# Cross-attention values on one Trainium2 core: four heads per product, 512 columns wide, with one set of split value weights

## The reference

```
qh = (q_in @ wq + bq)                      # h = norm(x)
kh = (kv_in @ wk + bk);  vh = (kv_in @ wv + bv)   # kv_in = context
kh = concat(kh, bias_k); vh = concat(vh, bias_v)  # one extra key per head
weights = softmax(qh kh^T / sqrt(128))
out = concat_heads(weights @ vh) @ wo + bo
```

## Time and profile before

| what | value |
|---|---|
| median of 3 runs | 1978.76 us (1978.57 to 1981.2) |
| the profiled execution's own time | 1977.81 us |
| its span | 1975.7 us |
| mean granted TensorE clock | 0.974 |
| TensorE busy | 1875.9 us, 95% |
| VectorE, ScalarE, GpSimd busy | 56%, 53%, 50% |

### The profile page before, as it was taken

One profiled execution on the slowest core, in us unless ns is written; L12 is line 12 of the kernel. 1 busy time (PEld: TensorE's weight loads), 2 busy tenths in 40 slices (PEclk: granted clock), 3 DMA queues, 4 the chain that ended last, 5 costly groups with the idle time before them and its releaser, 6 DMA issues.

```text
span 1975.7 us, 39304 instructions
## 1 busy us (share of the span) xinstructions
PE 1875.9 (95%) x15088; PEld 1551.0 (79%) x15088; DVE 1113.9 (56%) x2104; ACT 1044.2 (53%) x1945; POOL 996.6 (50%) x1140
## 2 busy tenths in 40 slices
PE   7999999988897899999999999999999998999999
PEld 5777779534454788899999999999999987977788
DVE  4566656389989654444454444454444455755654
ACT  3565543434343656665665656556566554345532
POOL 6777731366654543654544544545454434347630
PEclk9999999889998999999999999999999999999999
DMA  6000010000000222232232232232232210000000
GB/s 236 2 2 2 2 57 1 1 0 1 1 1 11 91 81 75 83 104 83 82 106 82 81 107 82 81 107 82 81 102 87 81 60 22 22 29 16 2 11 33
DMA packets 61847, 108.11 MB, mean 55 GB/s; under 512 B 7008, under 2 KB 42336, under 8 KB 60256
## 3 DMA queue, kind: packets, MB, share of 16 engines
q1 hardware_dynamic: 60784, 103.38, 16.7%
q10 hardware_dynamic: 880, 2.22, 0.3%
HBM read 103.47 MB, written 2.10 MB: 53 GB/s over the span
## 4 chain that ended last, share of the span: by engine, by line
PE 84%; DVE 7%; issue 4%; POOL 3%; ACT 2%; DMA 0%; DVEq 0%; SPq 0%; ACTq 0%; POOLq 0%
PE banks L862 18%; PE banks L891 9%; PE banks L934 9%; PE banks L627 7%; PE banks L644 7%; PE banks L466 7%; PE banks L923 6%; PE banks L904 4%; PE banks L475 3%; PE banks L548 2%; PE banks L523 2%; PE banks L505 2%; PE banks L534 2%; PE banks L912 1%; PE banks L460 1%
## 5 line engine op out<-in xcount | busy, mean ns | idle before, releaser
L1983 POOL TENSOR_TENSOR w_lo<-w2ring,w_hi 128x512 fp32r<-128x512 f32 x128 | 176.1, 1376 | 254.9 <-ACT w_hi L1128 254.9
L2067 POOL TENSOR_TENSOR wo_lo<-wo_ring,wo_hi 128x256 fp32r<-128x256 f32 x128 | 94.6, 739 | 254.6 <-ACT wo_hi L1337 254.6
L1808 DVE TENSOR_REDUCE nmax<-banks 128x4 f32<-128x260 f32 x128 | 54.3, 424 | 280.2 <-PE banks L904 280.2
L1794 DVE TENSOR_TENSOR v<-banks,dbv 128x512 f32<-128x512 f32 x128 | 88.5, 692 | 201.6 <-PE banks L891 200.7
L1337 ACT ACTIVATE wo_hi<-wo_ring 128x256 fp32r<-128x256 f32 x128 | 53.3, 417 | 197.6 <-PE banks L934 197.5
L934 PE MATMUL banks<-wo_hi,c_hi 128*128 128x256 f32 x512 | 145.5, 284 | 4.4 <-DVE c_lo L1801 4.4
L934 PE MATMUL banks<-wo_lo,c_hi 128*128 128x256 f32 x512 | 145.4, 284 | 0.0
L934 PE MATMUL banks<-wo_hi,c_lo 128*128 128x256 f32 x512 | 145.3, 284 | 0.0
L1324 ACT ACTIVATE k<-banks,cols 128x512 f32<-128x512 f32 x128 | 88.1, 688 | 79.4 <-PE banks L862 79.4
L923 PE MATMUL banks<-PT,v 128*128 128x128 f32 x1024 | 125.3, 276 | 3.4 <-issue 3.4
L923 PEld LDWEIGHTS banks<-PT,v 128*128 128x128 f32 x1024 | 120.3, 192 | 3.8 <-issue 3.8
(11 more groups left out here) (235 smaller groups left out, 5525.1 us busy)
## 6 DMA issues: line engine op xcount, KB each, us to landing
w2ring<-in_w SPq DMA_DIRECT2D x128, 384.0 KB, 4.1
b2ring<-in_b SPq DMA_DIRECT2D x128, 128.0 KB, 4.5
wo_ring<-in_wo SPq DMA_DIRECT2D x128, 128.0 KB, 4.3
mlp_w<-in_mlp SPq DMA_DIRECT2D x6, 1024.0 KB, 7.1
wl<-in_wres SPq DMA_DIRECT2D x1, 2688.0 KB, 9.0
X<-in_x_in SPq DMA_DIRECT2D x4, 512.0 KB, 11.1
wb<-in_wres SPq DMA_DIRECT2D x2, 1024.0 KB, 10.8
ctxT<-in_ctx_in SPq DMA_DIRECT2D x4, 512.0 KB, 19.8
```

The costliest lines, as they stand in the source:

```text
L1794: V.tensor_tensor(v2[:, :, 2 * half:2 * half + 2, :].rearrange("p s i d -> p i s d"), held(("v2", p, half))[:, :].rearrange("p (i s d) -> ...
L1983: G.tensor_tensor(w2_lo[:, n % 2, :], w2ring[:, n % HR, 0:2 * KT * P], w2_hi[:, n % 2, :].bitcast(f32), ALU.subtract).then_inc(S["l2_wlo"], 1)
L2067: G.tensor_tensor(wo_lo[:, n % 2, :], wo_ring[:, n % WR, :], wo_hi[:, n % 2, :].bitcast(f32), ALU.subtract).then_inc(S["l2_wolo"], 1)
```

## The change

Values are now computed for four heads at a time (HV = 4), in the iterations with n % 4 == 0. The moving operand is 512 columns wide, so that each of the four tiles of tokens fills one bank with six matmuls. v2 becomes four tensors, one per tile of tokens, two of them placed in memory that layer 2 leaves free. There is one set of wv_hi and wv_lo, for four heads, in the same memory as the two sets before. dbv is made four heads ahead rather than two. VectorE reads four banks in one iteration of two, and the waits are recounted.

```diff
+HV = 4
-        v2 = view(at("v2", A + 13584, 2 * TOK), "p (s t d) -> p s t d", s=2, t=NT)
+        v2 = [view(at(f"v2_{i}", w, HV * P), "p (s d) -> p s d", s=HV) for i, w in
+              enumerate((A + 13584, A + 14096, masks_at + 1024, masks_at + 1536))]
-        wv_hi, wv_lo = (view(at(n, M + 2048 + 1024 * i, 2 * KT * 2 * P, f32r), "p (s k h d) -> p s k h d", s=2, k=KT, h=2)
+        wv_hi, wv_lo = (view(at(n, M + 2048 + 1024 * i, KT * HV * P, f32r), "p (k h d) -> p k h d", k=KT, h=HV)
...
 TensorE, values(n)
-                        c, p = n // H2 % CHUNKS, n // 2
-                        pe.wait_ge(S["l2_wvlo"], n + 2)
-                        for half in range(2):
-                            b = take(pe, ("v2", p, half), "l2_v", 2 * p + half + 1)
-                            for i in (2 * half, 2 * half + 1):
-                                pairs = [(x, y, k) for x, y in SPLIT for k in range(KT)]
-                                for x, y, k in pairs:
-                                    last = mm(b[:, i % 2 * D:(i % 2 + 1) * D], (ctx_hi, ctx_lo)[x][:, c, k, i * P:(i + 1) * P],
-                                              (wv_hi, wv_lo)[y][:, p % 2, k].rearrange("p h d -> p (h d)"),
-                                              start=(x, y, k) == pairs[0], stop=(x, y, k) == pairs[-1])
+                        c, v = n // H2 % CHUNKS, n // HV
+                        pe.wait_ge(S["l2_wvlo"], n + HV)
+                        pairs = [(x, y, k) for x, y in SPLIT for k in range(KT)]
+                        for i in range(NT):
+                            b = take(pe, ("v2", v, i), "l2_v", NT * v + i + 1)
+                            for x, y, k in pairs:
+                                last = mm(b, (ctx_hi, ctx_lo)[x][:, c, k, i * P:(i + 1) * P],
+                                          (wv_hi, wv_lo)[y][:, k].rearrange("p h d -> p (h d)"),
+                                          start=(x, y, k) == pairs[0], stop=(x, y, k) == pairs[-1])
                             last.then_inc(S["l2_v_mm"], 1)
 TensorE, weigh(n)
-                        pe.wait_ge(S["l2_v"], 2 * (n // 2) + 2)
+                        pe.wait_ge(S["l2_v"], NT * (n // HV + 1))
-                            last = mm(out, v2[:, n % 2, i, :], PT2[:, n % 2, i].rearrange("p r q -> p (r q)"), start=True, stop=True)
+                            last = mm(out, v2[i][:, n % HV, :], PT2[:, n % 2, i].rearrange("p r q -> p (r q)"), start=True, stop=True)
 TensorE and VectorE, the loop
-                        values(n)
+                        if n % HV == 0:
+                            values(n)
 ScalarE, value_weights_hi(n)
-                    p = n // 2
-                    if p >= 2:
-                        act.wait_ge(S["l2_v_mm"], 2 * (p - 1))
+                    if n >= HV:
+                        act.wait_ge(S["l2_v_mm"], NT * (n // HV))
 VectorE, values(n)
-                        dve.wait_ge(S["l2_dbv"], n + 2)
+                        dve.wait_ge(S["l2_dbv"], n + HV)
-                        for half in range(2):
-                            dve.wait_ge(S["l2_v_mm"], 2 * p + half + 1)
-                            V.tensor_tensor(v2[:, :, 2 * half:2 * half + 2, :].rearrange("p s i d -> p i s d"),
-                                            held(("v2", p, half))[:, :].rearrange("p (i s d) -> p i s d", i=2, s=2),
-                                            dbv.unsqueeze(1).to_broadcast([P, 2, 2, P]), ALU.add).then_inc(S["l2_v"], 1)
+                        for i in range(NT):
+                            dve.wait_ge(S["l2_v_mm"], NT * v + i + 1)
+                            V.tensor_tensor(v2[i], held(("v2", v, i)).rearrange("p (s d) -> p s d", s=HV), dbv, ALU.add).then_inc(S["l2_v"], 1)
 GpSimd, bias_values(n)
-                        if n >= 2:
-                            pool.wait_ge(S["l2_v"], 2 * (n // 2))
-                        G.tensor_tensor(dbv[:, n % 2, :], ...
+                        if n >= HV:
+                            pool.wait_ge(S["l2_v"], NT * (n // HV))
+                        G.tensor_tensor(dbv[:, n % HV, :], ...
 GpSimd, start of cross2
                     for n in range(2):
                         bias_key(n)
+                    for n in range(HV):
                         bias_values(n)
 GpSimd, the loop
-                            if head + 2 < NH:
-                                bias_values(head + 2)
+                            if head + HV < NH:
+                                bias_values(head + HV)
```

More of the change, by code:

```diff
@@ L292, in build @@
         k2 = view(at("k2", A + 12544, 2 * NB * KX), "p (s b k) -> p s b k", s=2, b=NB)
-        v2 = view(at("v2", A + 13584, 2 * TOK), "p (s t d) -> p s t d", s=2, t=NT)
+        v2 = [view(at(f"v2_{i}", w, HV * P), "p (s d) -> p s d", s=HV) for i, w in
+              enumerate((A + 13584, A + 14096, masks_at + 1024, masks_at + 1536))]
         PT2 = view(at("PT2", A + 14608, 2 * NT * P), "p (s i r q) -> p s i r q", s=2, i=NT, r=2)
-        wv_hi, wv_lo = (view(at(n, M + 2048 + 1024 * i, 2 * KT * 2 * P, f32r), "p (s k h d) -> p s k h d", s=2, k=KT, h=2)
+        wv_hi, wv_lo = (view(at(n, M + 2048 + 1024 * i, KT * HV * P, f32r), "p (k h d) -> p k h d", k=KT, h=HV)
                         for i, n in enumerate(("wv_hi", "wv_lo")))
         P2 = view(at("P2", A + 15632, 2 * NT * SEQ), "p (s t k) -> p s t k", s=2, t=NT)
-        dbv = view(at("dbv", A + 16144, 2 * P), "p (s d) -> p s d", s=2)
+        dbv = view(at("dbv", A + 16144, HV * P), "p (s d) -> p s d", s=HV)
         E2 = view(at("E2", A + 25344, 2 * NT * KX), "p (s t k) -> p s t k", s=2, t=NT)
@@ L1130, in value_weights_hi @@
                 def value_weights_hi(n):
-                    p = n // 2
-                    if p >= 2:
-                        act.wait_ge(S["l2_v_mm"], 2 * (p - 1))
-                    A(wv_hi[:, p % 2, :, n % 2, :], view(w2ring[:, n % HR, 2 * KT * P:], "p (k d) -> p k d", k=KT), ACT.Copy)\
+                    if n >= HV:
+                        act.wait_ge(S["l2_v_mm"], NT * (n // HV))
+                    A(wv_hi[:, :, n % HV, :], view(w2ring[:, n % HR, 2 * KT * P:], "p (k d) -> p k d", k=KT), ACT.Copy)\
                         .then_inc(S["l2_wvhi"], 1)
@@ L1787, in values @@
                     def values(n):
[L1788 to L1789 removed]
+                        v = n // HV
+                        dve.wait_ge(S["l2_dbv"], n + HV)
                         if n:
                             dve.wait_ge(S["l2_pv"], n)
[L1792 to L1796 removed]
+                        for i in range(NT):
+                            dve.wait_ge(S["l2_v_mm"], NT * v + i + 1)
+                            V.tensor_tensor(v2[i], held(("v2", v, i)).rearrange("p (s d) -> p s d", s=HV), dbv, ALU.add).then_inc(S["l2_v"], 1)
                     def context(n):
@@ L1987, in value_weights_lo @@
                     pool.wait_ge(S["l2_wvhi"], n + 1)
-                    h = n // 2 % 2
-                    G.tensor_tensor(wv_lo[:, h, :, n % 2, :], view(w2ring[:, n % HR, 2 * KT * P:], "p (k d) -> p k d", k=KT),
-                                    wv_hi[:, h, :, n % 2, :].bitcast(f32), ALU.subtract).then_inc(S["l2_wvlo"], 1)
+                    G.tensor_tensor(wv_lo[:, :, n % HV, :], view(w2ring[:, n % HR, 2 * KT * P:], "p (k d) -> p k d", k=KT),
+                                    wv_hi[:, :, n % HV, :].bitcast(f32), ALU.subtract).then_inc(S["l2_wvlo"], 1)
                 def mixing_shift(c):
@@ L2078, in bias_values @@
                         pool.wait_ge(S[f"w2_in{n % HR}"], 32 * (n // HR + 1))
-                        if n >= 2:
-                            pool.wait_ge(S["l2_v"], 2 * (n // 2))
-                        G.tensor_tensor(dbv[:, n % 2, :], b2ring[:, n % HR, 0, :], b2ring[:, n % HR, 1, :], ALU.subtract).then_inc(S["l2_dbv"], 1)
+                        if n >= HV:
+                            pool.wait_ge(S["l2_v"], NT * (n // HV))
+                        G.tensor_tensor(dbv[:, n % HV, :], b2ring[:, n % HR, 0, :], b2ring[:, n % HR, 1, :], ALU.subtract).then_inc(S["l2_dbv"], 1)
                     updated(pool, EARLY - 1)
```

1 line of the change is left out of this document (removed).

## The result

The kernel after takes 1965.30 us in the median (1964.85 to 1966.06, 4 runs) against 1978.66 for the kernel before (1977.19 to 1981.20, 4 runs): ratio 0.9931, 95% interval 0.9915 to 0.9947. The direction was right; the forecast size was too small. The profiled execution took 1965.55 us, its span is 1963.7: 1.8 us between the two, where the kernel before has 2.1.

The account below looks back on a forecast made before the run. TensorE's matmuls were taken as the bound in layer 2's attention; -8.1 - 2.5 + 0.6 = -10.0 us gave 1967.8 us, or 1968.8 as median. Own range 1967 to 1971, 8 in 10 from 1966.3 to 1973.0.

Parts of the forecast that it names:

- Part 1: Value matmuls of layer 2: 24 of 512 columns replace 48 of 256 per four heads, -8.1 us over 32 sets.
- Rival B: Value matmuls: 512 columns cost two times 256, so part 1 is nothing; 1976.9 us, 5% together with the skill page's case.
- Part 2: Iterations without values: losing the value block delays nothing at PT, banks, additions, weights, loads or last iteration; priced at nothing.
- The cover of 1.2 us for PT: Iterations without values: `weigh` starts 1.2 us after its PT is ready, so no wait was priced.
- rival C: Iterations without values: PT becomes the bound and `weigh` waits, 1988.0 us at 0.6 us each; 4%, 2% more for smaller waits.
- At h = 2 VectorE's update of X must precede `project`: Part 2, iterations at h = 2: the update's place in the order is before the values, no delay found, nothing priced.
- SP's next load then depends on wv_lo rather than dbv and comes earlier: Part 2, value iterations: GpSimd's dbv moves two heads earlier and the next load comes earlier; priced at nothing.
- the median stood 0.95 above it: In the sum: 0.95 us from profiled execution to median, carried from 1967.8 us to the predicted 1968.8.
- Part 3: First chunk, n = 6: the 2.60 us wait and lower clock behind it go, a shorter wait comes at n = 8; -2.5 us.
- the new wait: Third query group of n = 8 waits for the first c_lo: 0.8 us, or 2.8 if xm slows beside GpSimd.
- Rival A: First chunk: the stall only moves, n = 8 idles and cools as n = 6 did, part 3 is nothing; 1971.3 us, 14%.
- Part 4: Start of layer 2: GpSimd makes dbv of heads 2 and 3 before w_lo(2), +0.6 us, between 0 and 0.9.

Follow-up runs that it names:

- e2: Kernel after with each tile's value matmuls in two halves of 256 columns into the same bank; 1976.65 us, ratio 0.9977.
- e6: Kernel after with three needless 128 x 496 copies on ScalarE ahead of PT from n = 16 on; 1987.66 us, ratio 1.0044.
- e3: Kernel before with VectorE's value additions of n = 6 ahead of the mixing; 1973.07 us, ratio 0.9961.
- e8: e4 with the second half of VectorE's mixing of chunk 3 moved from n = 6 to the end of n = 8; 1968.12 us, ratio 0.9947.
- e4: Kernel after with dbv of heads 2 and 3 made behind the low weights of these heads; 1965.41 us, ratio 0.9933.
- e9: e8 with the context parts of n = 12, 14, 16 ahead of the output and value weights of their own iteration; 1965.22 us, ratio 0.9931.
- e15: Kernel after with only the context parts of n = 12, 14, 16 moved ahead within their iteration; 1966.17 us, ratio 0.9936.
- e1: Kernel after, unchanged, run again against the kernel before; 1965.96 us, ratio 0.9927.
- e10: Kernel before with only the context parts of n = 12, 14, 16 moved ahead within their iteration; 1974.67 us, ratio 0.9981.
- e14: Kernel before, unchanged, a third further profiled execution on a third chip; 1982.54 us.
- e0: Kernel before, unchanged, run against itself; 1978.45 us, ratio 0.9996.
- e12: Kernel before, unchanged, one further profiled execution on a third chip; 1978.91 us.
- e5: e4 with context parts moved to n = 10, 12, 14 and half of chunk 3's mixing moved to the end of n = 8; 1966.95 us, ratio 0.9935.
- e13: Kernel before, unchanged, a second further profiled execution on a third chip; 1976.79 us.

## Why the prediction was right, and where it was wrong

- **Part 1, the matmuls: right.** 0.2286 us per 512 columns against 0.2282, 0.26 us per set in all 32, 8.3 us against 8.1; e2 gives them back. Rival B falls. The Trainium skill, "TensorE: Matmul & The Clock Gate", section "Back-to-back issue gap", would have 0.06 us per set by its isolated gap; the rows and e2 have 0.26.
- **Part 2: right but for two places.** Banks, additions, the single weight set and the last iteration cost nothing. The cover of 1.2 us for PT is 1.1 by e6, and it was never used up; rival C falls. "At h = 2 VectorE's update of X must precede `project` ... I found no delay there either" was wrong once: 0.7 us at n = 18, because one P ran into GpSimd's w_lo.
- **The step that failed** is the one that let a single execution of the kernel before stand for all: nothing was priced for what varies between executions. In the prediction's own terms it has two places. In part 2, "SP's next load then depends on wv_lo rather than dbv and comes earlier. All priced at nothing": the prediction didn't ask who waits for that load. At n = 14 of the kernel before it sets the length of TensorE's wait for ctx_lo, and that iteration took 16.98 to 19.36 us, in the mean of six executions 1.1 more than in the one that the sum was made from; the kernel after took 14.03 to 14.08. And in the sum, "the median stood 0.95 above it" carried the distance over as if it were the same after; the kernel after's profile lies 0.25 us above its own median. From the first scores on, the six executions of the kernel before took 1319.7 us in the mean, 1.9 more than the first, whose late start of layer 2 (657.86 us, the six have 655.49 to 658.28) hid its short stretch. Why the excess went with the change is open, as said above.
- **The 0.3 us outside the spans** (2.1 us before, 1.8 after) was no term of the sum, and nor was 0.7 at n = 18.
- **The range's lower end**, 1966.3, is 0.6 us below what its stated ends give (1978.76 - 8.4 - 3.5 = 1966.9). The measured 1965.3 lies under both.
- **Part 3: right for this pair of executions.** 2.7 us against 2.5, the new wait 1.25 between 0.8 and 2.8, at the third query group of n = 8 as named. Rival A would have needed the clock to fall at n = 8; it stays at its upper level. Since e3 and e8 show that the wait's length alone doesn't decide this, it may in part be luck that it stayed up here.
- **Part 4: right**, 0.5 us against 0.6, and e4 recovers 0.6.

That the earlier load keeps the wait at n = 14 short is read from the traces of both kernels; a run that delays the load in the kernel after, or one that brings it forward in the kernel before, wasn't made. Why the low clock behind layer 2 costs 2 to 3 us more in e2, e6, e8, e9 and e15 than in the kernel after stays open. The chip doesn't explain it, since e2 and e6 ran on the same chip as e1 and e4. e10 (352.4 us there) and e14 show that the kernel before has that loss in some executions too. Why e10 kept a spread of 6.7 us is open as well.

## What to carry to other kernels

Sum the terms by one execution, but look at the spread of the runs first. Where the runs of one kernel lie some us apart, as here (1975.3 to 1984.1), take several profiles of it before the sum and compare them by stretches: some waits end on something that varies, and a change may remove that loss together with the terms. When an instruction or a load becomes earlier, follow the chain behind it to TensorE, also where it looks idle. And before GpSimd's work is shifted, see what VectorE makes there: one short product of two SBUF operands behind a long GpSimd instruction is as late as that one's end.

## What the runs showed of the hardware

- The clock behind a wait of TensorE isn't set by the wait's length alone. At n = 14, waits of 1.94 to 1.96 us left it at 1.00 in five executions (the kernel after, e1, e2, e4, e6) and lowered it in a sixth (e8); waits of 2.36, 2.76 and 2.77 us lowered it (e0, e12, e14), and one of 2.77 us did not (e3).
- Such a fall cost 1.6 us beyond the wait: n = 14 of e8 took 15.65 us and that of the kernel after 14.08, with the same wait.
- The loss behind layer 2 varies by 2 to 3 us for the same code and the same waits: 348.2 to 348.4 us from n = 126 to the end in four profiles (the kernel after, e1, e4, e5), 350.3 to 351.5 in five others with the same instructions there (e2, e6, e8, e9, e15). A gain of 2 to 4 us far ahead can vanish in that.
- A VectorE product of 0.43 us with both inputs in SBUF took 1.39, 2.32 and 2.77 us behind or beside GpSimd's instructions, of 1.3 to 2.5 us in all (n = 18 of the kernel after, n = 12 of e5).
- A load of the same size, issued at the same point, lands 0.9 us later in one execution than in another (b2ring at 778.9: e13 and e14).
